# A decoder layer's self attention on one NeuronCore: merging two small maxima with a reduce instead of an elementwise maximum

## The reference

```python
def _L1_attn_ref(X, W_qkv, W_out):
    b, s, _ = X.shape            # 2, 1024, 256
    h, d = (16, 64)
    qkv = (X @ W_qkv).reshape(b, s, h, d, 3)
    q, k, v = (qkv[..., 0], qkv[..., 1], qkv[..., 2])
    scores = jnp.einsum('bqhd,bkhd->bhqk', q, k) / d ** 0.5
    weights = jax.nn.softmax(scores, axis=-1)
    attn = jnp.einsum('bhqk,bkhd->bqhd', weights, v)
    return attn.reshape(b, s, h * d) @ W_out
```

## Time and profile before

| | us |
|---|---|
| median of 3 runs | 2783.05 |
| lowest and highest of them | 2777.99, 2784.57 |
| the profiled execution | 2786.26 |
| its span, first to last instruction | 2784.5 |

### The profile page before, as it was taken

How to read it: one execution, slowest core, us unless ns; L and a number is a source line. 1 busy time by engine, 2 the same in 40 slices (tenths; PEclk the granted TensorE clock), 3 DMA queues, 4 the chain that set the end, 5 groups by cost and what they waited for, 6 DMA issues and landing times. The chain is left out here.

```text
span 2784.5 us, 42524 instructions
## 1 busy us (share of the span) xinstructions
PE 2063.7 (74%) x11308; PEld 1210.6 (43%) x11308; DVE 2220.6 (80%) x10063; ACT 1731.5 (62%) x5762; POOL 654.1 (23%) x343
## 2 busy tenths in 40 slices
PE   6233555766666757667576769999999998799997
PEld 3122334454545544555445433333333332565654
DVE  5999999999999999999999846666666665186668
ACT  3578888888888888888888224444444444222231
POOL 0000000000000000000000027887787788000000
PEclk9655556576676676656757669999999999799998
DMA  4833222343343432333333011111111110201100
GB/s 110 166 100 66 51 56 67 70 115 81 81 104 82 116 83 71 102 81 100 88 70 87 5 38 31 56 45 40 45 34 51 34 49 12 88 12 43 46 8 8
DMA packets 154021, 180.27 MB, mean 65 GB/s; under 512 B 20916, under 2 KB 128344, under 8 KB 153816
## 3 DMA queue, kind: packets, MB, share of 16 engines
q1 hardware_dynamic: 153816, 178.00, 25.5%
HBM read 138.08 MB, written 39.88 MB: 64 GB/s over the span
## 5 line engine op out<-in xcount | busy, mean ns | idle before, releaser
L1595 ACT ACTIVATE mix_cand<-mix_pre,mixer_cbuf 128x32 f32<-128x32 f32 x2048 | 592.9, 289 | 151.0 <-DVE mix_pre L1521 75.6
L1592 ACT ACTIVATE mix_cand<-mix_state,mixer_cbuf 128x32 f32<-128x32 f32 x2048 | 653.8, 319 | 28.2 <-DVE mix_state L1513 4.7
L1508 DVE SCALAR_TENSOR_TENSOR mix_prod<-mixer_keys,mixer_cbuf,mix_cand 128x65 f32<-128x65 f32 x2048 | 580.0, 283 | 55.9 <-ACT mix_cand L1595 48.6
L1521 DVE SCALAR_TENSOR_TENSOR mix_pre<-mixer_keys,mix_gap,mix_state 128x32 f32<-128x32 f32 x2048 | 523.5, 256 | 27.7
L1513 DVE SCALAR_TENSOR_TENSOR mix_state<-mix_cand,mixer_cbuf 128x32 f32<-128x32 f32 x2048 | 504.2, 246 | 0.1
L2048 POOL TENSOR_TENSOR self_psum<-self_psum,self_prob 128x1024 f32<-128x1024 f32 x192 | 452.5, 2357 | 138.2 <-ACT self_prob L1970 130.2
L2062 DVE TENSOR_REDUCE self_tops<-self_rough 128x2 f32<-128x1024 f32 x252 | 307.5, 1220 | 202.7 <-PE self_rough L1844 196.6
L1626 PE MATMUL mix_out<-all_ident,mix_state 128*128 128x128 f32 x504 | 150.8, 397 | 415.3 <-ACT mix_flat L1575 372.0
L1970 ACT ACTIVATE self_prob<-self_sco 128x1024 f32<-128x1024 f32 x256 | 261.4, 1025 | 314.9 <-PE self_sco L1857 279.3
L876 POOL TENSOR_TENSOR mix_st_norm_rstd<-mix_st_norm_var,mix_half 128x2 f32<-128x2 f32 x24 | 17.4, 725 | 1323.4 <-DVE mix_st_norm_var L869 1323.4
L1626 PEld LDWEIGHTS mix_out<-all_ident,mix_state 128*128 128x128 f32 x504 | 78.3, 196 | 497.8 <-ACT mix_flat L1575 421.2
(11 more groups left out here) (395 smaller groups left out, 3466.9 us busy)
## 6 DMA issues: line engine op xcount, KB each, us to landing
mixer_keys<-k_rows SPq DMA_DIRECT2D x256, 260.0 KB, 5.1
mix_early_w<-in_w_qkv SPq DMA_DIRECT2D x48, 384.0 KB, 4.0
kq_rows<-mix_early_row SPq DMA_DIRECT2D x96, 128.0 KB, 2.1
self_qk<-kq_rows SPq DMA_DIRECT2D x16, 768.0 KB, 4.8
aT_rows<-self_aT SPq DMA_DIRECT2D x32, 256.0 KB, 2.7
two_aT<-aT_rows SPq DMA_DIRECT2D x8, 1024.0 KB, 6.8
v_rows<-mix_early_row SPq DMA_DIRECT2D x48, 128.0 KB, 1.8
self_v<-v_rows SPq DMA_DIRECT2D x16, 384.0 KB, 3.5
```

The costliest lines, as they stand in the source:

```text
L1508: dve.scalar_tensor_tensor(prod[:, b, :], keys[:, h, b, s_, :], coef(NIB, h, s_, b), cand[:, b, s % 2, :], ALU.mult, ALU.mult, accum_out=g ...
L1521: dve.scalar_tensor_tensor(pre[b], keys[:, h, b, s_, NS:2 * NS], gap[:, b:b + 1], state[:, hp, sp_, b, :], ALU.mult, ALU.add).then_inc(pre ...
L1592: act.activation(cand[:, b, (s + 1) % 2, NS:2 * NS], state[:, hp, sp_, b, :], ACT.Copy, scale=cbuf[:, h, KEEP, b, s_:s_ + 1]).then_inc(kep ...
L1595: act.activation(cand[:, b, (s + 1) % 2, 0:NS], pre[b], ACT.Tanh, scale=cbuf[:, h, BETA, b, s_:s_ + 1]).then_inc(c_ready[b], 1)
```

## The change

In `join_tops` the elementwise maximum of two tensors, each 8 numbers per partition, becomes a maximum over an axis of one tensor with 16 numbers per partition. The view of `tops` is permuted so that the key half is its innermost axis, with 8 numbers between its two elements. The output, the wait ahead of it and the semaphore behind it are the same, and so is the order of the instructions on every engine: one DVE instruction in each of 32 places has another form.

```diff
             def join_tops(hp):
 
                 dve.wait_ge(rough_taken, hp * NROUGH + NROUGH)
-                dve.tensor_tensor(wide_top[:, :, 0:QT], tops[:, 0, :, :].rearrange("p t u -> p u t"),
-                                  tops[:, 1, :, :].rearrange("p t u -> p u t"), ALU.max).then_inc(top_ready, 1)
+                dve.tensor_reduce(wide_top[:, :, 0:QT], tops[:, :, :, :].rearrange("p k t u -> p u t k"), AX.X, ALU.max).then_inc(top_ready, 1)
```

## The result

The changed kernel takes 2758.64 us (median of 4 runs, 2755.41 to 2762.04) against 2782.95 us before: a ratio of 0.9916 with a 95% interval of 0.9894 to 0.9937, which is 17.5 to 29.5 us less.

The account below looks back on a forecast made before the run. PE was taken to bound the kernel, its waits standing behind the join. 18.95 us of idle time plus 2.2 us made 21.1, taking 2783.05 to 2762.0 us; own range 2756 to 2766, 8-in-10 range 2756 to 2771.

Parts of the forecast that it names:

- The bound: Self attention's steady stretch: PE busy 642.87 of 660.00 us sets the pace; its only wait, 18.5 us, is for the join.
- The cause: At 31 joins the two-SBUF-input maximum waits for POOL's running two-SBUF-input instruction; a one-input reduce would be free of POOL.
- The duration: The new join alone lasts between 160 and 280 ns, taken as 0.17 us by the old join alone.
- The size: At 31 joins PE gets back 18.95 us of idle time plus 31 x 0.07 = 2.2 us, together 21.1 us.
- The 0.2 us of slack: At the transpose the join is ready 0.20 or 0.19 us early, so it may take about 0.36 us.
- What is late next: After the join nothing else is late: lay_shift moves with the transpose, POOL has 134 us idle, ACT's POOL waits are for scores.
- The total: Whole kernel: the median of 2783.05 less 21.1 gives 2762.0 us, 0.76% faster.
- The second figure: Whole kernel, profiled execution: 2786.26 less 21.1 gives 2765.2 us.
- (a): At the join, POOL holds back a one-input reduce just as well, so the time is 2783; chance 0.06.
- (c): At the join, the reduce is let in only when POOL pauses: 55 us more, 2838; chance 0.02.
- (b): At the join, a longer reduce or eaten slack loses part of the gain: 10.5 us at 0.7 us, 2772; chance 0.07.

Follow-up runs that it names:

- pool16_old: Kernel before with its old join, POOL's self-attention instructions cut to 16 columns, rest of sums and normalised output left out: 2755.58 us, ratio 0.9914.
- pool_pow: Kernel before with its old join, POOL's self-attention instructions made powers of 12 or 6 columns: 2765.99 us against 2787.65, a single execution of each.
- late16: Changed kernel with one more reduce of 16 bf16 numbers ahead of the join, result unused: 2756.87 us, ratio 0.9929 to the kernel before.
- late256: Changed kernel with two more reduces of 128 bf16 numbers ahead of the join, results unused: 2761.64 us, ratio 0.9939 to the kernel before.
- the second session: Changed kernel without further edit, timed again over more rounds with a second profile: 2759.31 us against 2777.85 before, ratio 0.9934.
- copy: Changed kernel's reduce writing to a small tile, then a tensor_copy of 8 fp32 numbers to wide_top: 2777.40 us, ratio 1.0001 to the kernel before.

## Why the prediction was right

**The bound.** PE was named as the engine that sets the pace, with its only wait standing behind the join. It held: 19 us of idle time were named, and with them gone PE is busy in all of 42.96 us. PE waits for the join at the first place alone, for 1.9 us, where 1.85 was foretold.

**The cause.** The joins were said to end with POOL's instructions because of two SBUF inputs. Shown: the old join is fast when POOL's instructions are short (`pool16_old`), and the reduce is fast in the middle of long ones. The prediction's rule was too wide on both sides. Two SBUF inputs don't suffice for a wait: beside powers of the same length the old join ran free (`pool_pow`). And what the earlier trace rows were read to say, that one SBUF input makes an instruction free of POOL, fails for a copy: it held for the inversions, the `top` reduces and `lay_shift`, and for the new reduce, but not there. Had the change needed a copy, the same argument would have been wrong by the whole gain. That it came out right for the reduce rests on the case of a reduce from SBUF beside POOL, which the trace of before lacked, as the prediction says.

**The duration.** 0.17 us was taken, 0.174 measured; by inputs it would have been 164 ns, by outputs 282. The inner axis of two elements and the stride cost nothing that shows. The size taken was that of the old form, so its closeness is in part luck, but anything up to 0.37 us would have given the same time.

**The size.** The term of 21.1 us measured 21.4 and 21.2 by the turn-to-turn time of the two profiles, and 21.0 without the first 20 us of it. Both parts of it are confirmed: two half units lost 1.37 us, of which 1.24 was recorded as idle, and 0.07 at each transpose was the difference between the modelled end of `attend` and the moment from which PE can go on. The 0.2 us of slack were there: a join of 0.25 us costs nothing (`late16`), and one of 0.56 us costs 0.19 us where PE takes it up after 0.13 (`late256`), which puts the limit at 0.37.

**What is late next.** Nothing was, in the half units: `lay_shift` moved with the transpose, and the time that POOL waits for ACT over the whole stage fell from 155.1 us to 133.5, by what the stage lost in length. ACT's waits ascribed to POOL, 33.4 us, hardly moved, 31.9 us, and with POOL shortened the stage got no faster, so they were not on the path.

**The total.** 2762.0 was forecast and 2758.64 measured, within its own range of 2756 to 2766. The missing 3 us aren't explained by the change: the second session gave 18.5 us instead of 24.3. The second figure was further off: for the profiled execution 2765.2 was forecast, and it took 2755.41. Between the two profiles the span fell by 30.8 us, of which 21.4 lie turn to turn, 6.4 ahead of the first transpose (1651.66 to 1645.23) and 3.0 behind the last (448.3 to 445.4). The self attention's end has the same length in both, so these 3.0 are in the second layer, which the prediction expected to keep its length. No instruction was changed there, and its length, counted from its first matmul, varies from 406.5 to 414.0 us over the profiles of all kernels here. The profiled execution of before was slower than each of its timed runs. With such scatter outside the stage, it is in part luck that the medians agree to 3 us; it isn't luck that the term does.

**The rivals.** (a), held back all the same, and (c), let in only when POOL pauses, are excluded by the spread of 173 to 176 ns. (b), a partial loss, needed a join of more than 0.37 us. Two readings behind (c) were wrong and bore on nothing else. The 31 joins are 16 in first halves and 15 in second halves, not 15 and 16, which would make its price some 56 us instead of 55. And the longest join wasn't passed over at the seam of two additions. The earlier trace rows show the two merged; taken by itself, the second has started before the join:

```profile
1673.25 2.35 POOL L2048 TENSOR_TENSOR self_psum<-self_psum,self_prob 128x1024 f32<-128x1024 f32 x1
```

The join starts at 1673.48, 0.23 us into this addition, and waits for the rest of it. It is the longest because it met its addition earliest, not because it waited for two.

## What to carry to other kernels

When one short instruction of a single shape is recorded with durations that differ by a factor of ten, suspect a wait, and let its end tell for whom: here another engine's instruction had ended 0.02 to 0.03 us earlier, in all 31 places. Where VectorE works beside long additions or products of GpSimd on SBUF, try small VectorE steps on the way to TensorE as reduces, or with an operand in PSUM: those ran free here, while an elementwise instruction with two SBUF inputs, and a copy from SBUF to SBUF, each waited up to 2 us for 8 numbers. What GpSimd computes matters too, since beside its powers the elementwise form ran free. Before pricing such a step, work out when its consumer could start at the earliest: here 0.37 us cost nothing, and what lay beyond was paid at each of the 31 joins. And don't add up recorded durations of neighbouring instructions: look at when the next one starts.

## What the runs showed of the hardware

- A tensor_copy of 8 fp32 numbers from SBUF to SBUF waits for POOL's additions and products (median 0.83 us instead of 0.17, its end 0.03 us after that of POOL's instruction), although it has one input (`copy`).
- A maximum with two SBUF inputs isn't held back by a power on POOL of 2.27 us over 12 columns or of 1.32 us over 6 (0.17 us in each of 31 places, `pool_pow`). The Trainium skill, "SBUF — State Buffer", section "SBUF: two separate sides", has the pair of ports taken for the whole instruction; that fits the additions over 1024 columns and the products over 512, and doesn't fit the powers, where the measurement decides.
- Reduces that follow each other on DVE without a wait overlap in the record: of 128 numbers they start 0.20 us apart with 0.28 us recorded (`late256`), of 16 numbers 0.09 apart with 0.17 (`late16`).
- A reduce of 16 numbers to 8 per partition over an inner axis of two takes 0.174 us (the changed kernel), an elementwise maximum of 8 numbers 0.166 to 0.168 (`pool16_old`).
